# First cross attention with heads divided by GpSimd and a mixed order of TensorE, with a reworked opening and block order of the expert stage

## The reference

```
T = Q @ K.T / sqrt(16) + bias ; masked -> -1e9 ; A = softmax(T) ; out = (A @ V) @ WO + b
s1,i1 = top8(q1 . keys1) ; s2,i2 = top8(q2 . keys2) ; fs,pk = top8(s1 + s2)
y = sum_k gelu(x . down[fi_k]) * relu(fs_k) * up[fi_k]
```

## Time and profile before

| | us |
|---|---|
| runs | 2230.22, 2232.72, 2230.97 |
| median | 2230.97 |
| the profiled execution | 2233.26, span 2231.5 |

### The profile page before, as it was taken

How to read it: one execution, slowest core, us unless ns; L and a number is a source line. 1 busy time by engine, 2 the same in 40 slices (tenths; PEclk the granted TensorE clock), 3 DMA queues, 4 the chain that set the end, 5 groups by cost and what they waited for, 6 DMA issues and landing times. The chain is left out here.

```text
span 2231.5 us, 45916 instructions
## 1 busy us (share of the span) xinstructions
PE 2169.8 (97%) x18243; PEld 1464.3 (66%) x18276; DVE 1686.2 (76%) x4495; ACT 814.7 (37%) x1943; POOL 177.8 (8%) x427
## 2 busy tenths in 40 slices
PE   7999999999999999999999999999989999999998
PEld 3555554446756756775555555556679989898997
DVE  6898896876576576536877787877698989888885
ACT  4888882311312302303554554545322111211110
POOL 4552201000000000000000000000000000000000
PEclk9999999999999999999999999999999999999999
DMA  5011104000000003001000000001200000000000
GB/s 179 24 42 44 28 9 156 1 1 1 1 1 1 1 0 114 1 1 50 2 1 1 1 1 1 1 1 58 95 1 2 2 11 2 1 11 2 1 11 11
DMA packets 24166, 48.65 MB, mean 22 GB/s; under 512 B 5009, under 2 KB 13457, under 8 KB 22929
## 3 DMA queue, kind: packets, MB, share of 16 engines
q1 hardware_dynamic: 23952, 45.71, 6.2%
HBM read 37.57 MB, written 2.10 MB: 18 GB/s over the span
## 5 line engine op out<-in xcount | busy, mean ns | idle before, releaser
L2416 PE MATMUL banks<-work,big 128*128 128x128 f32 x2016 | 248.9, 277 | 2.2 <-PEq L378 1.5
L623 ACT ACTIVATE work<-banks,work 128x512 f32<-128x512 f32 x256 | 174.6, 686 | 202.3 <-DVE work L742 202.3
L2416 PEld LDWEIGHTS banks<-work,big 128*128 128x128 f32 x2016 | 242.3, 193 | 7.8 <-issue 3.4
L1121 PE MATMUL banks<-big,work 128*128 128x256 f32 x1024 | 241.3, 379 | 3.6 <-issue 3.3
L1045 PE MATMUL banks<-big,work 128*128 128x512 f32 x512 | 226.6, 596 | 0.3 <-DMA big<-in_B_val 0.2
L2509 ACT ACTIVATE work<-banks 128x512 f32<-128x512 f32 x126 | 75.2, 597 | 407.4 <-PE banks L2416 404.3
L1121 PEld LDWEIGHTS banks<-big,work 128*128 128x128 f32 x1024 | 195.4, 191 | 33.6 <-issue 1.9
L1939 ACT ACTIVATE work<-work 128x512 f32<-128x512 f32 x256 | 181.0, 711 | 0.0
L1045 PEld LDWEIGHTS banks<-big,work 128*128 128x128 f32 x512 | 95.6, 190 | 114.0 <-issue 112.6
L742 DVE TENSOR_REDUCE work<-banks 128x2 f32<-128x1024 f32 x128 | 150.5, 1218 | 7.7 <-PE banks L475 7.7
L1343 DVE CUSTOM_DVE_ANT_0 work<-banks,work 128x512 f32<-128x512 f32 (+3 forms) x128 | 57.7, 488 | 121.5 <-PE banks L1061 109.2
(11 more groups left out here) (252 smaller groups left out, 3801.3 us busy)
## 6 DMA issues: line engine op xcount, KB each, us to landing
work<-work SPq DMA_DIRECT2D x152, 32.0 KB, 2.0
big<-in_bias SPq DMA_DIRECT2D x16, 256.0 KB, 4.7
big<-in_B_val SPq DMA_DIRECT2D x8, 512.0 KB, 6.6
big<-in_B_out SPq DMA_DIRECT2D x1, 4096.0 KB, 18.3
big<-in_D_downT SPq DMA_DIRECT2D x4, 1024.0 KB, 5.0
big<-in_D_up SPq DMA_DIRECT2D x1, 4096.0 KB, 15.7
wc<-in_ctxT SPq DMA_DIRECT2D x1, 2048.0 KB, 7.8
wab<-in_L_ffn_w_q SPq DMA_DIRECT2D x1, 2048.0 KB, 9.7
```

Of the source, the lines that this page charges most:

```text
L623: eng.activation(prob[:, n % NS * PAIR + j, :], SB[n % 2][:, j, :], ACT.Exp, bias=low[:, n % NS, j:j + 1], accum_out=rowsum[:, n % NS, j:j ...
L1121: last = eng.matmul(XO[qt // 2][:, qt % 2 * D:(qt % 2 + 1) * D], spread[:, c % NG, qt * P:(qt + 1) * P], w_out[:, c, :], start=False, stop ...
L2416: last = eng.matmul(HP[n % 2][:, q * P:(q + 1) * P], down[:, (n * NJ + q) * KC + kc, :], xnT[par][:, kc, :], start=(kc == 0), stop=(kc == ...
```

## The change

- `mult` is gone: no `invert`, `inverses`, `normalise`, no row sums from the exponentials. ScalarE copies the group's raw product with its sums (`take_o`) into one of two buffers. SP gathers both the heads and the sums (`gather_heads`, 8 transfers a group), and GpSimd divides two groups at a time (`weigh_heads`: an inverse by three Newton steps, then the product). The last pair is divided in the second stage.
- `slot(n)` has another order of jobs; the filler matmuls of steps without a job are gone.
- In steps whose job is not `q`, `k` or `v`, `weigh` comes ahead of the second `turn_probs`. The loops are one step shorter.
- Experts: the last `update` of the third stage is made on VectorE at the beginning of the expert block; ScalarE stages tile 1 at the end of the third stage. The opening turns the picks of tile 0 first, compares tile 1 after the hidden block 4 (into banks 2 and 3) and does two parts of the choice for tile 1. In a turn, PICK is 7 and not 5, `weights(i, 0)` stands behind the second hidden block, the parts of the choice are spread as `PARTS` says, and split and the first two `onehots` of the next tile follow `apply(i, 7)`.

```diff
+def gather_heads(eng, m, heads, whole, sums, g):
+    A = A_
+    for j in range(A.group):
+        r, at = (g % 2 * A.group + j) * A.dk, A.strip * j + A.dk
+        eng.dma_start(sums[r:r + A.dk, :], heads[at:at + A.dk, :]).then_inc(m["A.sums_moved"][g % 2], 16)
+    for j in range(A.group):
+        r, at = (g % 2 * A.group + j) * A.dk, A.strip * j
+        eng.dma_start(whole[r:r + A.dk, g // 2, :], heads[at:at + A.dk, :]).then_inc(m["A.compacted"][g], 16)
+def weigh_heads(eng, m, pair, whole, sums, inverse, product, step):
+    A = A_
+    b, kc = divmod(pair, A.groups // 2)
+    for moved in m["A.sums_moved"]:
+        eng.wait_ge(moved, 16 * A.group * (pair + 1))
+    if pair:
+        eng.wait_ge(m["A.weighted"], pair)
+    n = (1 + 3 * NEWTON) * pair
+    eng.tensor_scalar(inverse.bitcast(I32), sums.bitcast(I32), -1.0, INVERSE_SEED, ALU.mult, ALU.add).then_inc(step, 1)
+    for k in range(NEWTON):
+        eng.wait_ge(step, n + 3 * k + 1)
+        eng.tensor_tensor(product, inverse, sums, ALU.mult).then_inc(step, 1)
+        eng.wait_ge(step, n + 3 * k + 2)
+        eng.tensor_scalar(product, product, -1.0, 2.0, ALU.mult, ALU.add).then_inc(step, 1)
+        eng.wait_ge(step, n + 3 * k + 3)
+        eng.tensor_tensor(inverse, inverse, product, ALU.mult).then_inc(step, 1)
+    eng.wait_ge(step, n + 3 * NEWTON + 1)
+    for g in (2 * kc, 2 * kc + 1):
+        eng.wait_ge(m["A.compacted"][g], 16 * A.group * (b + 1))
+    eng.tensor_tensor(whole[:, kc, :], whole[:, kc, :], inverse, ALU.mult).then_inc(m["A.weighted"], 1)
...
-    OUT_AT = (5, 6, 10, 12)
+    OUT_AT = (11, 13, 14, 15)
     def slot(n):
         b, i = divmod(n, PER)
         more = b + 1 < B
-        if i % QT == 3:
-            return ("mult", (n - 7) // QT) if n >= 7 and (n - 7) // QT < B * G else None
-        if i in (0, 1) and b < B:
+        if i in (0, 2) and b < B:
             return ("q" if i == 0 else "k", b, 1)
         if n == 5:
             return ("const",)
         if i in OUT_AT and 0 < b < B:
             return ("out", b - 1, OUT_AT.index(i))
-        if more and i in (2, 13):
-            return ("k" if i == 2 else "q", b + 1, 0)
-        if more and i in (8, 9):
-            return ("x", b + 1, i - 8)
-        if more and i in (4, 14):
-            return ("v", b + 1, 0 if i == 4 else 1)
+        if more and i in (4, 12):
+            return ("k" if i == 4 else "q", b + 1, 0)
+        if more and i in (9, 10):
+            return ("x", b + 1, i - 9)
+        if more and i in (6, 8):
+            return ("v", b + 1, 0 if i == 6 else 1)
...
-                def compact(b, g):
-                    eng.wait_ge(dve_took, TOOK[("mult", G * b + g)])
+                def gather(b, g):
+                    eng.wait_ge(o_taken, G * b + g + 1)
                     if b >= 2:
                         eng.wait_ge(job_made, MADE[("out", b - 2, QT - 1)])
-                    for j in range(GH):
-                        r = (g % 2 * GH + j) * DK
-                        eng.dma_start(whole[b % 2][r:r + DK, g // 2, :], onorm[STRIP * j:STRIP * j + DK, g % 2, :]
-                                      ).then_inc(compacted[g], 16)
+                    eng.wait_ge(weighted, (G * b + g) // 2)
+                    gather_heads(eng, m, oT[g % 2], whole[b % 2], sums, g)
...
+                    if b >= 2:
+                        eng.wait_ge(row_step, ROWS * (b + 1))
+                        weigh_heads(eng, m, 2 * b - 3, whole[b % 2], sums, mm, bt, m["A.newton_step"])
+                    if b >= 2:
+                        eng.wait_ge(weighted, 2 * b - 2)
                     for t in range(QT):
                         fold_bias(eng, b, t, fold_step, fold_at(b, t) - FOLD, mm, bt)
+                    eng.wait_ge(fold_step, fold_at(b, QT - 1))
+                    weigh_heads(eng, m, 2 * b - 2, whole[(b - 1) % 2], sums, mm, bt, m["A.newton_step"])
                     if b + 1 < B:
+                        eng.wait_ge(weighted, 2 * b - 1)
                         fold_rows(eng, b + 1)
+                weigh_heads(eng, m, 2 * B - 3, whole[B % 2], sums, mm, bt, m["A.newton_step"])
+                weigh_heads(eng, m, 2 * B - 2, whole[(B - 1) % 2], sums, mm, bt, m["A.newton_step"])
...
-                def inverses(g):
-                    eng.wait_ge(rinv_ready, g + 1)
-                    bank_free(eng, ("mult", g))
-                    for qt in range(QT):
-                        for j in range(GH):
-                            last = eng.matmul(MB[STRIP * j:STRIP * (j + 1), qt * P:(qt + 1) * P],
-                                              rinv[:, g % 2, qt * GH + j:qt * GH + j + 1].to_broadcast([P, STRIP]),
-                                              ident[:, :], start=True, stop=True)
-                    last.then_inc(job_made, 1)
...
-                        for g in range(G):
-                            eng.wait_ge(compacted[g], 16 * GH * (b + 1))
+                        eng.wait_ge(weighted, 2 * b + 2)
...
-                    if 5 < n <= LAST and slot(n) is None:
-                        sem_, count = took([slot(k) for k in range(n) if slot(k) is not None][-1])
-                        eng.wait_ge(sem_, count)
-                        keep_busy(MB, 1)
-                    if 1 <= n <= LAST:
+                    heavy = slot(n) is not None and slot(n)[0] in ("q", "k", "v")
+                    if heavy and 1 <= n <= LAST:
                         turn_probs(n - 1, 1)
                     if n >= 3 and (n - 3) // 2 < LAST // 2:
                         weigh((n - 3) // 2, (n - 3) % 2)
+                    if not heavy and 1 <= n <= LAST:
+                        turn_probs(n - 1, 1)
                     if n > LAST:
...
-                    if n % QT == 0 and n >= 2 * QT:
-                        eng.wait_ge(rinv_ready, n // QT - 1)
-                    one, at = prob[:, n % 2, j, :], n % QT * GH + j
-                    eng.activation(one, one, ACT.Exp, bias=low[:, n % 2, j:j + 1], scale=-1.0,
-                                   accum_out=rowsum[:, n // QT % 2, at:at + 1]).then_inc(p_ready, 1)
+                    one = prob[:, n % 2, j, :]
+                    eng.activation(one, one, ACT.Exp, bias=low[:, n % 2, j:j + 1], scale=-1.0).then_inc(p_ready, 1)
                 def take_o(g):
                     eng.wait_ge(av_made, 4 * (g + 1))
-                    if g:
-                        eng.wait_ge(dve_took, TOOK[("mult", g - 1)])
-                    eng.activation(oT, OB, ACT.Copy).then_inc(o_taken, 1)
+                    if g >= 2:
+                        eng.wait_ge(compacted[(g - 2) % G], 16 * GH * ((g - 2) // G + 1))
+                        eng.wait_ge(m["A.sums_moved"][g % 2], 16 * GH * (g // 2))
+                    eng.activation(oT[g % 2], OB, ACT.Copy).then_inc(o_taken, 1)
...
-                def invert(g):
-                    eng.wait_ge(p_ready, GH * QT * (g + 1))
-                    if g >= 2:
-                        eng.wait_ge(dve_took, TOOK[("mult", g - 2)])
-                    eng.reciprocal(rinv[:, g % 2, :], rowsum[:, g % 2, :]).then_inc(rinv_ready, 1)
-                def normalise(g):
-                    eng.wait_ge(job_made, MADE[("mult", g)])
-                    eng.wait_ge(o_taken, g + 1)
-                    if g >= 2:
-                        eng.wait_ge(compacted[(g - 2) % G], 16 * GH * ((g - 2) // G + 1))
-                    eng.tensor_tensor(onorm[:, g % 2, :], MB, oT, ALU.mult).then_inc(dve_took, 1)
...
-    SELECT, PICK, START_PICK = 3, 5, 4
+    SELECT, PICK = 3, 7
...
+                turn_picks(0)
                 for n in range(2, NB):
                     hidden(0, 0, n)
                     if n == 2:
                         turn_x(1)
-                    if n == START_PICK:
-                        turn_picks(0)
-                compare(1, 1)
+                    if n == SELECT + 1:
+                        compare(1, 1)
...
-                        if n != SELECT + 1:
+                        if n == 1:
+                            weights(i, 0)
+                        if n and n != SELECT + 1:
...
-                stage_tile(eng, m, 1)
+                picks(0)
                 for n in range(2, NB):
                     hidden(0, 0, n)
-                    if n == START_PICK:
-                        picks(0)
-                select(1, 1)
+                    if n == 2:
+                        take_x(1, 1)
+                    if n == SELECT + 1:
+                        take_sims(1)
...
+                def last_update():
+                    eng.wait_ge(c_out.sem, c_out.at(B - 1, QT))
+                    eng.tensor_tensor(c_y, bank[6][:, 0:D], c_bo, ALU.add).then_inc(c_added, 1)
+                    eng.wait_ge(c_added, 1)
+                    xt = x[:, NT - 1, :]
+                    eng.scalar_tensor_tensor(out=xt, in0=c_y, scalar=m["gates"][:, 5:6], in1=xt, op0=ALU.mult, op1=ALU.add
+                                             ).then_inc(c_added, 1)
+                last_update()
```

(13 more changed lines are left out.)

117 lines of the change are left out of this document (55 added, 62 removed).

## The result

The changed kernel takes 2200.86 us (median of 4, 2198.74 to 2203.26), the kernel before 2230.59 beside it: ratio 0.9865, 95% interval 0.9848 to 0.9882. Forecast was 2205.0, range 2196 to 2219. The profiled execution took 2201.63 (2233.26 before).

The account below looks back on a forecast made before the run. TensorE, busy 97% of the span, was taken as the bound, with other engines' chains setting its gaps. Savings of 11.6 (attention), 2.0 (tail), 1.0 (border), 9.9 (opening) and 1.5 (last turns) made 26.0 us: forecast 2205.0, range 2196 to 2219.

Parts of the forecast that it names:

- Steps of the attention: First attention: `weigh` fills the gap in light steps, a 0.42 us wait for VectorE's copy appears; 11.6 us saved.
- All of them lie in the 1.28 us gap, so alone they bring nothing: First attention: removing inverses, their multiply, the exponential's accumulator output and fillers saves nothing by itself.
- rival 1: First attention: the clock falls in the empty steps, which lose their filler; 48 us slower, 2253; chance 0.08.
- The tail: End of first attention, from step 63 to the second stage's first matmul: 2.0 us saved, bounds 0 and 4.
- rival 2: First attention: GpSimd's division is late, 12 us in two batches, 2229, about level; chance 0.05.
- "Zero" for SP's queue: First attention: gathers wait for GpSimd on SP's queue, but the moves behind them are needed 8 us later or more; no cost.
- The border: Third stage to experts: the last update leaves VectorE's end of the stage, so experts start 1.0 us earlier.
- The opening: Expert stage's start: first `spend` at 42.9 us instead of 52.8, 9.9 us saved, bounds 3 to 11.6.
- Rival 3: Expert opening: turn 0 gives half, held by the load of `up` or weights against `apply`; 5 us less, 2210; chance 0.17.
- what paces turn 0: Expert opening: VectorE's chain to the last `apply` of turn 0 ends at 42.6 us, TensorE's at 41.9.
- The last stretch: Experts after the first `spend`: later turns keep their length, the last turns save 1.5 us, bounds 0 and 4.
- Rival 4: First attention: the mixed order brings nothing; the attention gives 3 us instead of 13.6, 2216; chance 0.12.

Follow-up runs that it names:

- the attention part alone: Kernel before with only the attention hunks of the change (division on GpSimd, mixed order, no inverses or fillers), expert stage as before: 2216.25 us, ratio 0.9930.
- the version with halved copies: Changed kernel with each transposed pair copied out by ScalarE and VectorE, one bank each, scores and minima handed over head by head: 2198.08 us, ratio 0.9843.
- the longer division: Changed kernel with six steps of the Newton iteration on GpSimd instead of three: 2245.14 us, ratio 1.0062.
- The two halves: Changed kernel with each turn's first weights put back: 2236.70 us (single execution); or with VectorE's old order and picks back from turn 1 on: 2218.28 us.

## Why the prediction was right, and where not

*Steps of the attention*: right. Starts of the scores in the changed kernel are apart by 4.04 (forecast 4.06) for empty after light, 4.83 (4.85) with the output product, 4.36 (4.34) and 3.94 (3.91) with x, 4.42 (4.42) output after heavy, 5.69 (5.70) heavy after light, 5.34 to 5.53 (5.46) after VectorE-paced ones, 3.79 to 3.89 (3.87) and 4.10 to 4.20 (4.15). The wait for VectorE's copy is 0.34, not 0.42. Sums: batches 1 and 2 76.3 each (76.5), batch 3 65.8 against 70.9: 5.1 (5.0; my 70.6 and 75.5 counted one step more), batch 0 4.0 (3.4), in all 12.5 (11.6). Batch 0 has the early fall of the clock in both traces, so there the figure is in part luck: the trace of the attention part alone, without the fall, has 77.5 us where the changed kernel has 80.2. The step is the cycle of one pair of banks, filled, emptied, filled, emptied; the version with halved copies, whose empty steps come to 3.86, shows that the copies are in that cycle.

*"All of them lie in the 1.28 us gap, so alone they bring nothing"*: half right. Inverses, multiply and sums brought nothing (226.97 us with and without them). The fillers lay in the gap as well, but they held the clock: without them and without the new order 14.3 us are lost. I asked only whether the new empty steps would hold it (they do), not what the old ones would do.

*The clock* (rival 1): out, by every step at full clock in the changed kernel behind the first ones. The danger was real, though: in the old order, without filler, it fell. The Trainium skill, "TensorE: Matmul & The Clock Gate", Part 4: PE-mode transpose, states the rule that I weighed, that a transpose does not count as activity in the way that a product does. The runs speak against it: two transposes in place of a product kept the clock as well as the product, 2211.97 and 2213.21 against 2227.50 with neither. The measurement decides for this kernel, with the gap that the filler breaks up as a rival that no run tried.

*The tail*: 1.9 (2.0), with another make-up: 1.47 us of wait in step 64, since VectorE had an update and statistics of x (319.84 to 321.17) and the four minima before its copy at 323.59. With the old order it is 16.0 us where it is 16.5 with the new one.

*GpSimd* (rival 2): priced at zero and right. The division took 12.3 (13.4), the slack was 4.2 (2.5). My argument that its durations "did not move beside VectorE in rows 3 and 4" was not in the rows, which show different stretches of time; in the changed kernel a product takes 1.28 us while VectorE is 87% busy (100 to 200 us). "Zero" for SP's queue held as well, but the longer division shows that queue as the next thing to be late.

*The border* 1.3 (1.0), right.

*The opening* 9.3 (9.9): right in size, not in what bounds it. First `spend` 43.5 after the stage's start (42.9), first weights at 19.7 (20.3), turn 0 at 16.0 (15.9) behind 0.86 us of waiting for `up`, VectorE's wait 4.8 (4). Rival 3 (half of it) is out. But my account began with "VectorE sits idle 7.46 us until the picks are turned", and that is no cause: with the picks late the stage is as fast. First weights stood at 19.4 before and at 19.7 after. What changed is from there to the first `spend`: 33.4 then, 23.9 now. Ranking began before turn 0 and the next tile's one-hots moved behind its last `apply`, so TensorE's waits of 4.20 (picks) and 1.71 (`spend`) went, and with them 1.7 us of the fall of the clock at 1639.8. The other 1.9 is a hidden block that now stands ahead of the first weights, in the place of the old waits of 1.20 and 0.73 (comparison, issue). That the late ranking made the 4.20 us is read from its releaser; it was not tried alone.

I also had VectorE as what paces turn 0 (42.6, TensorE 41.9). It does not: from the stage's start to the first `spend` TensorE waits 0.32 at the border, 0.86 for `up` and 0.71 for ScalarE's copy ahead of the comparison of turn 0, never for VectorE, and is busy 41.96 of 43.54 us. My sum for TensorE was 1.6 short: a hidden block takes about 1.86 and not 1.8 there, and the 0.71 was not in it. That two sums with these faults came out 0.6 from the measured time is luck in part.

*The last stretch* 6.9 (1.5): this step failed: "The later turns keep their length: VectorE's work is the same, in another order, and none of its results becomes later than its user." They became 0.33 us shorter, in 13 turns (from the second `turn_picks` to the last but one) 4.1 us (504.33 against 500.28). I had only asked whether a result comes too late, not whether one had been late before. TensorE's weight loads and matmuls of the old turn, which I had not opened since the matmul rows show no wait:

```profile
2075.83 1.86 PEld L2416 LDWEIGHTS banks<-work,big 128*128 128x128 f32 x16
2077.86 1.59 PEld L2443 LDWEIGHTS banks<-big,work 128*128 128x128 f32 x8 [0.17 <-DVE work L2592]
```

```profile
2075.86 2.03 PE L2416 MATMUL banks<-work,big 128*128 128x128 f32 x16
2077.86 2.00 PE L2443 MATMUL banks<-big,work 128*128 128x256 f32 x8
```

and the same place after:

```profile
2049.42 3.33 PEld L2450 LDWEIGHTS banks<-big,work 128*128 128x128 f32 x16
2049.53 3.62 PE L2450 MATMUL banks<-big,work 128*128 128x256 f32 x16
```

The first weights of `spend` are normally loaded before the block ahead of it ends (2049.42 for 2049.53). In the old turn they waited for VectorE's last `apply`, so `spend` began 2.00 us after the hidden block and not 1.87: 0.13 of the 0.33. The two halves bear this out: with VectorE's old order it is 2.00 again (1936.03 to 1938.03), with the first weights back and VectorE's new order 1.87. Another 0.18 lies in the order `spend`, weights, `spend`, which took 4.34 us from 2077.86 to the next hidden block at 2082.20, where two `spend` blocks in a row take 3.46 and a block of weights elsewhere 0.70. This second part is read from one trace; how the 0.33 divides between the two moves can't be said, because each move alone makes turns longer. The last two turns gave the other 2.8 (forecast 1.5 for them): TensorE's idle in them went from 1.05+1.85 to 0.78+1.03, as these rows of the end show, and 1.7 us at half clock are gone; the 1.05 us before the last picks I had overlooked.

```profile
2160.46 3.72 PE L2450 MATMUL banks<-big,wab 128*128 128x256 f32 x16 [0.78 <-DVE wab L2603]
2165.21 1.57 PE L2440 MATMUL banks<-wc 128*128 128x64 bf16 x48 [1.03 <-DVE wc L2591]
```

*Rival 4* (the order brings nothing, 2216) is out by the 12.3 us above. In sum: between the two profiled executions 31.7 us went where 26.0 was forecast, and 5.4 of the 5.7 us more are the last stretch; by the medians it was 29.7.

## What to carry to other kernels

Where a step fills, empties, fills and empties one pair of banks, write down that cycle: what fills its gaps is free, whatever ends it last is the next wait, and a second engine on the same copy shortens it as long as the copy does not stand inside another chain. Filler that lies in a gap is not free to take out: look at the clock row of a version without it, in the old order and in the new. And when judging that a reordering costs nothing, look in the weight-load rows too for results that were already late; orders of two engines are one edit, to be costed together.

## What the runs showed of the hardware

- Transposes as filler held the granted clock as products did (3.16 of 4.00 us busy, clock 1.00, from 300 to 304 us); without filler, at 2.79 of 4.00, it stayed full from 284 to 300 us and then fell to 0.50, with no gap above 1.21 us. A fall in the opening of the attention comes and goes between kernels whose code there is the same (mean clock from 28 to 60 us 0.89 with the change, 1.00 with its attention part alone).
- The four score products, which use 16 rows each of separate strips, end close together: with a handover behind each, the first minimum still starts 1.16 us after the scores (189.28 to 190.44), where one handover for all four gave 1.21 (153.09 to 154.30 in the earlier trace rows).
- Two copies of 512 columns cost VectorE 0.60 each from start to start and one of 1024 1.14; ScalarE 0.49 each and 0.90.
- GpSimd's operation on int32 words took 0.62 us, as its float ones of 128x512 with constant operands did; the product 1.28, and the one with an operand for each partition 1.56 (L1596).
